# Spreading the early threshold search over two of every three chunk slots in a GNN and mixture-of-experts layer

## The reference

```python
def _L0_gnn_ref(h, adj, simlar, W_proj, b_proj, W_gcn, b_gcn):
    sim = jnp.tanh(adj * simlar)                       # called with simlar = adj
    filt = sim * (adj > 0).astype(sim.dtype)
    vals, idx = jax.lax.top_k(filt, T)                 # T = 350, row by row
    nnz = jnp.sum(filt != 0, axis=1)
    keep = jnp.arange(T)[None, :] < nnz[:, None]
    new_adj = jnp.zeros_like(filt).at[rows, idx].set(jnp.where(keep, vals, 0.0))
    h2 = jnp.tanh(h @ W_proj + b_proj)
    return jax.nn.relu(new_adj @ (h2 @ W_gcn) + b_gcn)

def _L0_ffn_ref(x, Wg, bg, W1, b1, W2, b2):            # E = 8 experts, K = 2, H = 512
    gate_scores = jnp.einsum('bsd,ed->bse', x, Wg) + bg
    topk_scores, topk_idx = jax.lax.top_k(gate_scores, K)
    combine = ...                                      # softmax of the two, one-hot over experts
    for e in range(E):
        h = jax.nn.relu(jnp.einsum('bsd,hd->bsh', x, W1[e]) + b1[e])
        out = out + combine[..., e:e + 1] * (jnp.einsum('bsh,dh->bsd', h, W2[e]) + b2[e])

x = x + _L0_gnn_ref(_layernorm(x), adj, adj, ...)
x = x + _L0_ffn_ref(_layernorm(x)[None], ...)[0]
```

## Time and profile before

| | |
|---|---|
| median of 3 runs | 498.88 us (494.01 to 499.02) |
| the profiled execution | 498.55 us, its span 496.8 us |
| PE busy | 405.6 us (82%) |
| DVE busy | 361.9 us (73%) |
| ACT busy | 324.0 us (65%) |
| POOL busy | 224.5 us (45%) |
| mean granted TensorE clock | 0.931 |
| DMA | 97.08 MB, mean 195 GB/s |
| SP's issue of the first tile load | 301.1 us |
| first matmul of the experts (L1575) | 309.7 us |

### The profile page before, as it was taken

How to read it: one execution, slowest core, us unless ns; L and a number is a source line. 1 busy time by engine, 2 the same in 40 slices (tenths; PEclk the granted TensorE clock), 3 DMA queues, 4 the chain that set the end, 5 groups by cost and what they waited for, 6 DMA issues and landing times.

```text
span 496.8 us, 7360 instructions
## 1 busy us (share of the span) xinstructions
PE 405.6 (82%) x2144; PEld 232.5 (47%) x2144; DVE 361.9 (73%) x952; ACT 324.0 (65%) x329; POOL 224.5 (45%) x315
## 2 busy tenths in 40 slices
PE   2896999989889899999999999588578779687600
PEld 2453533334434334544554444466357668576500
DVE  4999958678999999969799998296356545354326
ACT  4577999899678879999998995153144344253300
POOL 7249965240217008144054883644744545535510
PEclk9998999989799999999999999888879999988955
DMA  8629889894658568776766982622234333210059
GB/s 277 245 97 413 334 278 324 304 353 150 245 214 252 194 222 296 294 292 240 289 214 239 312 301 49 107 54 56 98 96 88 85 56 78 63 40 30 22 177 335
DMA packets 54898, 97.08 MB, mean 195 GB/s; under 512 B 34165, under 2 KB 41386, under 8 KB 46658
## 3 DMA queue, kind: packets, MB, share of 16 engines
q1 hardware_dynamic: 43584, 79.40, 47.7%
q0 software_dynamic: 6560, 14.88, 9.6%
q10 hardware_dynamic: 4706, 2.23, 1.5%
HBM read 80.00 MB, written 12.27 MB: 186 GB/s over the span
## 4 chain that ended last, share of the span: by engine, by line
PE 43%; DVE 23%; issue 10%; ACT 9%; another core or an unknown queue 7%; DMA 6%; SPq 1%; ACTq 1%; POOL 0%; POOLq 0%; DVEq 0%
PE bank L1487 23%; ACT tbuf L1235 5%; PE bank L1601 5%; DVE marks L950 3%; PE bank L1602 3%; PE bank L1575 2%; PE bank L1577 2%; PE bank L1576 2%; DVE marks L947 2%; DMA tbuf<-expert_rows 2%; DVE rowbf L802 2%; DVE tbuf L1136 2%; DMA xres<-in_x 2%; DVE abuf L1144 1%
## 5 line engine op out<-in xcount | busy, mean ns | idle before, releaser
L1487 PE MATMUL bank<-tbuf,g_sb 128*128 128x512 f32 x512 | 242.4, 619 | 8.3 <-ACT g_sb L1249 5.2
L1487 PEld LDWEIGHTS bank<-tbuf,g_sb 128*128 128x128 f32 x512 | 95.6, 197 | 115.1 <-issue 98.9
L1235 ACT ACTIVATE tbuf<-abuf 128x2048 f32<-128x2048 f32 x64 | 121.5, 1898 | 13.1 <-DMA abuf<-in_adj_tiles 10.4
L1239 ACT ACTIVATE tbuf<-tbuf 128x2048 f32<-128x2048 f32 x64 | 122.3, 1911 | 2.0
L709 POOL DMA_INDIRECT routed_rows<-aug,slots x64 | 79.1, 1236 | 79.9 <-DVE base L930 62.0
L727 POOL DMA_INDIRECT expert_rows<-abuf,xmeta x72 | 70.5, 979 | 73.0 <-DVE abuf L1144 58.5
L950 DVE SCALAR_TENSOR_TENSOR marks<-abuf,marks 128x2048 bf16<-128x2048 int32 x32 | 76.4, 2387 | 1.6 <-DMA abuf<-in_adj_tiles 0.5
L1136 DVE SCALAR_TENSOR_TENSOR tbuf<-bank,tbuf 128x512 f16<-128x512 f32 x72 | 46.9, 682 | 37.2 <-ACT tbuf L1334 19.9
L1601 PE MATMUL bank<-w2hl,tbuf 128*128 x288 | 58.1, 288 | 15.5 <-issue 10.8
L1334 ACT ACTIVATE tbuf<-bank 128x512 f16<-128x512 f32 x72 | 41.0, 605 | 44.7 <-remote 27.3
L1602 PE MATMUL bank<-w2hl,tbuf 128*128 x288 | 54.4, 228 | 8.5 <-issue 8.5
(11 more groups left out here) (250 smaller groups left out, 438.0 us busy)
## 6 DMA issues: line engine op xcount, KB each, us to landing
abuf<-in_adj_tiles SPq DMA_DIRECT2D x64, 1024.0 KB
wstage<-in_w POOLq DMA_DIRECT2D x24, 256.0 KB, 6.4
tbuf<-expert_rows SPq DMA_DIRECT2D x8, 512.0 KB, 7.2
out<-xres ACTq DMA_DIRECT2D x8, 256.0 KB, 6.2
routed_rows<-pad SPq DMA_DIRECT2D x9, 130.0 KB
expert_rows<-abuf,xmeta POOLq DMA_INDIRECT x72
routed_rows<-aug,slots POOLq DMA_INDIRECT x64
abuf<-routed_rows SPq DMA_TRANSPOSE x40
```

What stands on the lines that cost most here:

```text
L1235: act.activation(tbuf[:, n % NBUF, :, :], abuf[:, n % NBUF, :, :], ACT.Square).then_inc(s_sq, 1)
L1239: act.activation(tbuf[:, n % NBUF, :, :], tbuf[:, n % NBUF, :, :], ACT.Tanh).then_inc(s_t, 1)
L1487: last = pe.matmul(ps_feat[ib % 2][:, :], g_sb[:, c, :], tbuf[:, buf, cc, :], start=(c == 0), stop=(c == C - 1))
```

## The change

The 15 search steps no longer stand in consecutive slots. `SEARCH` lists their slots: 20, 21, 23, 24, 26, 27, 29, 30, 32, 33, 35, 36, 38, 39, 41. So `TIE` goes from 35 to 42, and with it the mask from 36 to 43, the copy from 37 to 44, and `write_features` from 42 to 49. The fifth and sixth block to be routed (blocks 0 and 5) begin in slots 50 and 54, where they began in 47 and 51; the seventh and eighth stay. `FIRST` goes from 58 to 61. W1's pieces are split in slots 10, 12, 14, 16, 18, 44, 46 and 48, where it was 11, 13, 15, 17, 19, 21, 23 and 25. POOL loads and prepares the last piece, and writes the bias row, after its third scatter.

```diff
-    WAT = [2 + i if i < NPC else 11 + 2 * (i - NPC) for i in range(2 * NPC)]
+    WAT = [2 + i for i in range(NPC)] + [10, 12, 14, 16, 18, 44, 46, 48]
-    START = [19, 27, 35, 43, 47, 51, 58, 65]
+    START = [19, 27, 35, 43, 50, 54, 58, 65]
...
-    TIE = STEP0 + STEPS
+    SEARCH = [STEP0 + 3 * b // 2 for b in range(STEPS)]
+    TIE = SEARCH[-1] + 1
...
-            for j in range(NPC):
+            for j in range(NPC - 1):
                 take_last_row(j)
-                if j + 2 < NPC:
+                if j + 2 < NPC - 1:
                     first_pair(j + 2)
-            bias_row()
             for i, b in enumerate(ORDER):
+                if i == 4:
+                    first_pair(NPC - 1)
+                    take_last_row(NPC - 1)
+                    bias_row()
                 if i:
                     scatter(i - 1, routed)
...
-                if STEP0 < n <= TIE:
-                    raise_threshold(early, 0, n - STEP0 - 1)
-                if STEP0 <= n < TIE:
-                    count_candidates(early, 0, n - STEP0)
+                if n - 1 in SEARCH:
+                    raise_threshold(early, 0, SEARCH.index(n - 1))
+                if n in SEARCH:
+                    count_candidates(early, 0, SEARCH.index(n))
...
-                if STEP0 <= n < TIE:
-                    total_candidates(early, 0, n - STEP0)
+                if n in SEARCH:
+                    total_candidates(early, 0, SEARCH.index(n))
```

## The result

The changed kernel took 492.49 us (median of 20 runs, 487.88 to 498.6), the kernel before 496.51 us beside it (20 runs, 493.45 to 499.68). The ratio is 0.9904 with a 95% interval of 0.988 to 0.9928. A median here is of all runs, while a ratio leaves out those over 1.5% above the fastest of their kernel, so it is not the quotient of the two medians. The forecast was 500.0 us in a range of 494 to 506, so it was wrong in its sign as well. Of the 7.5 us between forecast and median, 2.0 lie in where the sum began: at 498.55 us, where the kernel before took 496.51 in 20 runs. The trace of the changed kernel has a span of 487.1 us against 496.8. It is of a run 3.5 us under its kernel's median, and that of the kernel before of one 2.0 us above, so the two spans lie further apart than the medians.

The account below looks back on a forecast made before the run. It took DVE to bound the stream to 204.9, then PE, and the sixth scatter's landing the hand-over. 498.55 + 0.6 (later tile 0, after 1.2 us stream gain) + 0.8 (clock) = 499.95, so 500.0 us, range 494 to 506.

Parts of the forecast that it names:

- its sign: Whole kernel: forecast slower, 500.0 us against 498.55 us for the profiled kernel before.
- What bounds the kernel: Stream: DVE bounds 117.9 to 204.9, then PE; after the change DVE bounds from slot 43, near 97% busy.
- The stream: Slots 21 to 49: 8.9 us of DVE work moves later, only vanishing waits gain; net 1.2 us, last mark at 306.4.
- The ceiling of 2.7 us: DVE's true slack in the stream: waits of 1.9 + 0.8 us, the most that the stream could gain.
- W1's pieces: Pieces before the search: five stand one slot earlier, absorbed by DVE's wait at 117.88; cost and give nothing.
- rival 2: Slots 43 to 61: coupled stall, two or three new waits delay the assignment 4 us; 504, or 507 with clock; chance 0.24.
- The hand-over: Stream to experts: sixth scatter at 293.1, SP's first load at 307.3, tile 0 at 310.3, 0.6 us later than before.
- Rival 3: Hand-over: the move is hidden, tile 0 starts with the stream's end, 1.2 us earlier; 497.4 us; chance 0.08.
- The clock: PE idles some 3 us ahead of tile 0 and may restart slower: priced at 3.3 us, a quarter (0.8 us) summed.
- The rest unchanged: Experts: 36 tiles follow with work and order unchanged, so the shift at tile 0 is carried to the end.
- Rival 1: Stream and first tiles: DVE relieved, 496.1; 491 to 494 if slow issue at 316.2 to 323.0 vanishes; chance 0.18 with milder form.
- over 1% faster: Whole kernel: outcome needing the second half of rival 1, the vanished slow issue; chance 0.16 with what was overlooked.

Follow-up runs that it names:

- padded pair: Kernel before and changed kernel, each with 68 one-element matmuls added at PE's very start: 497.06 us (ratio 1.0026) and 493.58 us (ratio 0.9977).
- three of four slots: Changed kernel with search in three of every four slots, fifth and sixth block as before: 446.86 us (0.9925), and 498.41 us (0.9978) on the 496 kind.
- slot 56: Seventh block begun in slot 56, not 58, in the kernel before: 509.29 us (1.0291); in that with three of four slots: 508.22 us (1.0179).

## Why the prediction was wrong, point by point

**What bounds the kernel.** That DVE's queue was the bound up to 204.9, and the landing of the sixth scatter at the end, both hold. That the bound goes from PE to DVE behind slot 42 doesn't: from 210.1 to 299.9 PE is busy 89.20 of 89.80 us, and DVE 82.64, which is 92% where I had named 97%. PE's gap was foreseen in its place and taken at some 3 us; it is 7.9, since DVE's last mark, for which PE's last counts wait, came at 302.8 and not at 306.4.

**The stream, taken at 1.2 us of gain.** The place was right: slot 43 on DVE begins at 211.0 (213 forecast). The size was not. The last mark ends at 302.8 (306.4 forecast, 307.6 before), a gain of 4.7 us; in the runs of the 450 kind it is 5.6. The ceiling of 2.7 us was wrong. From the mark of chunk 20 to that of chunk 63 the changed kernel's DVE needed 188.9 us and the kernel before 195.5 (450 kind), with 1.8 us less busy and 4.8 us less idle. The listed waits fell from 7.6 to 3.1 us, and 2.4 us of that are the wait for "issue" ahead of `write_features` (3.0 to 0.6; 2.9 to 0.6 on the 496 kind). I had called these 2.9 us work in another form, and left them out of the ceiling; most of them went. Instructions got shorter too, which I had not allowed for: the count's first one (`cand`) takes 160 ns where it took 244, its second (`rowbf`) 558 for 635. Why, no run shows.

**W1's pieces, at nothing in the sum.** This step failed. Those that stand a slot earlier do "cost and give nothing", nearly (0.4 us); it is the three that I moved to slots 44 to 48. Against the profiled kernel before of the 450 kind, the pieces alone end the last mark 5.2 us earlier (304.4 for 309.6), of which 2.3 us stand there from the mark of chunk 0 on and are that run's start: 2.9 us are left. Search and blocks without the pieces are, corrected in the same way, 1.1 us late, and the whole change 5.3 us early: beside the other parts the pieces are worth 6.4 us. The times say the same, 3 and 6.1 us. I had moved the pieces' 3.2 us out of the tight slots and back in again in slots 44 to 48. What came back was only 2.3 us (from the mark of chunk 42 to that of chunk 49 the gain falls from 7.2 to 4.9), and what was saved between the marks of chunks 20 and 26 was 4.5 us.

**The new waits (rival 2).** They didn't come in the change. The three waits at L813 are 1.4 us together, and the one at L899 is 1.3. Rival 2 had the point from which it decides at an assignment of 294.5 to 297; it came at 289.6. Search and blocks without the pieces are that rival, in fact: waits of 8.3 us in these two places, assignment at 295.6 and 1.8% slower.

**The hand-over.** The path was right, and the times came within a microsecond, in part by luck: SP's first load 307.3 forecast, 306.7 measured; tile 0 310.3 forecast, 311.2 measured. The errors cancel: POOL began at 290.4 instead of 293.1; from there to SP's load it was 16.3 us and not 14.2, since the indirect DMAs took 1.9 and 2.5 us here and there; and from the load to tile 0 it was 4.5 us and not 3. That last wait ends on the landing of the tile's second DMA (`xmeta`), which SP issues 1.6 us behind the first; I had read the first one's burst. Moving the blocks alone confirms the mechanism at a larger size: 9.5 us at tile 0. Rival 3 (hidden) falls with it, since the wait of 7.90 us ends on the tile's load.

**The clock, 0.8 us in the sum.** After 7.9 us without work PE runs at 1.2 GHz until 317.1. Tile 0 to tile 1 takes 4.7 us for 2.4, and tile 1 to tile 2 3.3 for 2.7, so the clock cost 2.8 us (1.6 on the 450 kind). The Trainium skill (TensorE: Matmul & The Clock Gate, HAM oscillation) told that it would be throttled, and the trace agrees. The 3.3 us of the prediction were near that, if a little too high, and the quarter of it in the sum was too low.

**The rest unchanged, "so I carry the shift to the end".** This is the step that turned the sign. On the 450 kind it holds exactly: the shift of 1.5 us at tile 1 is 1.5 us at the last tile, and the measured 0.5% slower is about what my sum gives (1.4 us forecast, 1.7 us in the spans). That is luck in part: tile 0 is 0.2 us early where I had 0.6 late, and the clock took 1.6 us where I had 0.8. On the 496 kind, which is that of the runs I had, the experts are not a fixed block. Their slow stretch of 6.8 us goes with the seventh scatter beside PE, and in the change it is gone. Tile 2 is 4.3 us late, tile 3 2.9 us early, and the medians differ by 4.0 us. Rival 1 had this in words, "if the shifted scatter leaves this stretch, up to 5 us vanish: 491 to 494", which is where the time came out (2 us of it by the kernel before, which was faster than the sum had it). I gave over 1% faster 0.16, with the argument that "the loads move later and into it". That looked at where the loads go and not at where the seventh scatter goes. This scatter hangs on the last marks: it began 3.3 us behind the last one before (307.6, 310.9), and 2.1 us behind it now (302.8, 304.9). With my last mark of 306.4 it would have begun at about 309 and PE at 310.3, so they would still have met. By this reckoning, which no run tests, it took the 4.7 us of the stream, which my ceiling excluded, together with a first tile that doesn't follow, to put the scatter into PE's gap. Then both failed steps were needed to turn the sign: the first moved the scatter, and the second left out that the scatter matters.

Of the 9.7 us between the two spans, 6.8 arise behind tile 3, in later stretches that differ from run to run; in the padded pair nothing is gained there (5.0 us at tile 3, 3.1 in the spans, 3.5 in the medians). The medians' 4.0 us are the figure to trust.

## What to carry to other kernels

Before a shift is carried to the end of the program, look at what runs beside the stretches in which an engine issues slowly: here such a stretch moved with a neighbour's DMAs, and its absence outweighed the edit. A moved step is worth what stands at the hand-over (here the first tile load) and not what its own queue gains; price each part of a change alone, since here (450 kind) the part that looked neutral carried the gain, and the rest paid it back. A wait without a named releaser is no proof of work that must be done: most of the 2.9 us that I had read so went away. And when runs of one kernel can lie 10% apart on different occasions, a ratio holds only for the kind on which it was taken: this change is 1% faster on one and 0.5% slower on the other.

## What the runs showed of the hardware

- The same kernel took 450 us on some occasions and 496 us on others, on one chip too. The difference lies in the experts alone, where PE and DVE get an instruction every 0.7 us or slower in stretches of 2 to 16 us.
- On the 496 kind, the long stretches (6 us and more) begin 1.4 to 5.2 us behind the first of POOL's eight indirect DMAs of a block, and last 2 to 8 us beyond the last of them. For the seventh block's, the stretch is there in the three kernels whose PE began the experts 1.2 us ahead of them (the kernel before, with three of four slots, and padded), and in the two where they were moved beside later tiles. It is absent in the three whose PE began 5 to 6 us behind them (the change, twice, and padded), but shorter ones (4.0 and 4.9 us) are there in the two with slot 56, whose PE also began 5.8 us behind. Each long stretch also has a 16 KB packet of PE's instruction queue up to 3.2 us ahead of it. Stretches of 3 to 4 us (at 404.5 and 431.6 in the kernel before) stand with no block's scatter beside them. On the 450 kind the same DMAs cost PE nothing, with a packet amid them (317.5) too. What distinguishes the occasions is open.
- The Trainium skill (Runtime: NRT & Kernel Launch, Instruction fetch mechanics) says that each sequencer fetches its instructions in blocks of 16 KB through a DMA queue of its own, and that the cost of a crossing is mostly hidden. PE's queue, with its 21 packets of 16 KB, fits the first half; the traces' other instruction queue has 27 packets of 8 KB, so a block there is smaller or comes in two. On the 450 kind the second half fits as well. On the 496 kind a supply that is slowed by POOL's indirect DMAs would explain most of the rows, but no run here shows it.
